# Moving the second half's layer-norm work behind the first index list

## The reference

```python
h = h + attn(_layernorm(h), ...)
x = _layernorm(h).reshape(-1, D)                 # second layer norm
gate_logits = x @ gate_weight.T                  # 16 experts
top_vals, top_idx = jax.lax.top_k(gate_logits, 2)
routing_w = jax.nn.softmax(top_vals, axis=-1)
mask = any(top_idx == arange(E))
hid = jax.nn.silu(einsum('td,efd->tef', x, w1))  # per chosen expert
h_mean = sum over the tokens of an expert / counts
y_mean = einsum('ef,edf->ed', h_mean, w2)
out = einsum('tk,tkd->td', routing_w, y_mean[top_idx])
```

## Time and profile before

| | us |
|---|---|
| median of 3 runs | 421.34 |
| lowest, highest | 420.61, 424.37 |
| profiled execution, its own span | 501.4 |
| first gather starts, in that span | 200.03 |
| first expert product starts | 252.03 |

### The profile page before, as it was taken

One profiled execution on the slowest core, in us unless ns is written; L12 is line 12 of the kernel. 1 busy time (PEld: TensorE's weight loads), 2 busy tenths in 40 slices (PEclk: granted clock), 3 DMA queues, 4 the chain that ended last, 5 costly groups with the idle time before them and its releaser, 6 DMA issues.

```text
span 501.4 us, 7310 instructions
## 1 busy us (share of the span) xinstructions
PE 397.6 (79%) x1929; PEld 269.9 (54%) x1930; DVE 311.4 (62%) x827; ACT 218.1 (43%) x423; POOL 205.3 (41%) x231
## 2 busy tenths in 40 slices
PE   8999999998898987554591404589987877899984
PEld 7888888886898974423440101244433433344552
DVE  3598888888788999543530101577744543577884
ACT  3334555445232666536350101456644443567320
POOL 2011111115400998757467775400066666610510
PEclk9999999998998996756587556799999788999998
DMA  6206533322209350647312111100291111100029
GB/s 182 66 1 164 139 86 109 102 80 82 81 1 262 98 140 2 193 140 212 106 57 52 54 52 43 31 0 2 54 331 47 37 47 42 47 16 1 1 73 251
DMA packets 53020, 43.68 MB, mean 87 GB/s; under 512 B 20686, under 2 KB 45980, under 8 KB 52732
## 3 DMA queue, kind: packets, MB, share of 16 engines
q1 hardware_dynamic: 44276, 32.09, 22.3%
q0 software_dynamic: 4416, 9.05, 6.5%
q10 hardware_dynamic: 4296, 2.15, 1.6%
HBM read 34.86 MB, written 8.42 MB: 86 GB/s over the span
## 4 chain that ended last, share of the span: by engine, by line
PE 47%; DVE 19%; issue 12%; another core or an unknown queue 10%; ACT 6%; POOL 3%; DVEq 2%; ACTq 0%; POOLq 0%
PE P L662 16%; PE P L935 14%; PE P L867 6%; ACT P L1265 4%; DVE BIG L1712 3%; DVE H L1828 2%; PE P L905 2%; PE P L1062 2%; PE P L697 2%; PE P L655 1%; POOL XN L597 1%; DVE arena L1504 1%; POOL arena L594 1%; PE P L688 1%
## 5 line engine op out<-in xcount | busy, mean ns | idle before, releaser
L1712 DVE TENSOR_TENSOR BIG<-BIG,P 128x512 f32 x138 | 95.0, 688 | 115.9 <-issue 75.1
L935 PE MATMUL P<-w1T,arena 128*128 x276 | 142.4, 652 | 12.0 <-DVE BIG L1712 8.7
L935 PEld LDWEIGHTS P<-w1T,arena 128*128 128x128 f32 x276 | 52.6, 209 | 67.1 <-issue 66.4
L1254 ACT COPY arena<-P 128x384 f32<-128x384 f32 (+1 forms) x48 | 22.4, 467 | 119.6 <-remote 50.4
L1265 ACT ACTIVATE P<-P 128x512 f32<-128x512 f32 x138 | 72.8, 580 | 1.6 <-PE P L935 1.5
L614 POOL DMA_INDIRECT XN<-table,arena x60 | 58.1, 968 | 30.1 <-issue 18.1
L614 POOL DMA_INDIRECT arena<-table,arena x42 | 39.7, 946 | 57.9 <-PE P L935 40.8
L557 POOL TENSOR_TENSOR rs<-ve,mhalf 123x4 f32<-123x4 f32 x16 | 17.6, 1098 | 101.9 <-DVE ve L1356 101.9
L1103 ACT ACTIVATE arena<-P 128x492 f32<-128x492 f32 x48 | 27.9, 583 | 50.6 <-PE P L662 50.5
L614 POOL DMA_INDIRECT BIG<-table,arena x36 | 34.6, 960 | 24.7 <-remote 12.4
L905 PE MATMUL P<-ident,XN 128*128 128x128 f32 x60 | 11.4, 304 | 41.6 <-issue 35.3
(11 more groups left out here) (242 smaller groups left out, 639.7 us busy)
## 6 DMA issues: line engine op xcount, KB each, us to landing
arena<-kpad SPq DMA_DIRECT2D x16, 492.0 KB, 4.0
XN<-in_L_ffn_w SPq DMA_DIRECT2D x1, 4096.0 KB
arena<-in_x SPq DMA_DIRECT2D x16, 224.0 KB
table<-XN SPq DMA_DIRECT2D x4, 896.0 KB
BIG<-table SPq DMA_DIRECT2D x1, 2048.0 KB
out<-H SPq DMA_DIRECT2D x8, 224.0 KB
out<-H ACTq DMA_DIRECT2D x8, 224.0 KB
BIG<-table SPq DMA_DIRECT2D x1, 1024.0 KB
```

Of the source, the lines that this page charges most:

```text
L935: mm = nc.tensor.matmul(bank[:, :], stat, w1T[:, bass.ds(e * FF, FF)], start=True, stop=True)
L1254: nc.scalar.copy(GTs[:, bank, 0:count * SLOT], PT[:, 0:count * SLOT]).then_inc(GT_ready, 1)
L1712: v.tensor_tensor(at, at, bank[:, :], ALU.add).then_inc(esum_step, 1)
```

## The change

Statistics, moments and bias of quarters 2 and 3 leave the first list's part of DVE's program and stand in and behind the searches of quarters 2 and 3. The bias of quarter 0 (`shift(0)`) moves from ahead of the first search to behind it. POOL computes the factors of quarters 2 and 3 between gathers, ahead of gathers 8 and 18, and the eight rows of quarter 2 that it normalised go to ACT. ACT normalises all 32 rows of quarters 2 and 3 in the second list's part. PE's `ranks(0)` moves one n up, `ranks(1)` and `totals` two.

```diff
-NORM_POOL = (8, 8, 8, 0)
+NORM_POOL = (8, 8, 0, 0)
+        RSTD_AT = (8, 18)
@@ POOL
-            def norms(g):
+            def rstd_of(g):
                 pool.wait_ge(ve2_ready, g + 1)
                 qb = slice(g * QB, (g + 1) * QB)
                 nc.gpsimd.tensor_tensor(rs2[0:T, qb], ve2[0:T, qb], mhalf[0:T], ALU.pow).then_inc(rstd2, 1)
+
+            def norms(g):
                 pool.wait_ge(rstd2, g + 1)
...
-            norms(0)
+            rstd_of(0)
...
+            rstd_of(1)
+            norms(0)
             norms(1)
-            norms(2)
-            norms(3)
...
+                    if n in RSTD_AT:
+                        rstd_of(QA + RSTD_AT.index(n))
                     if n in paces:
@@ PE
                 x2_transposes(n)
-                if n == 11:
+                if n == 10:
                     ranks(0)
-                if n == 15:
+                if n == 13:
                     counts_behind(1, 0, 2)
+                if n == 14:
+                    ranks(1)
+                    totals(1, 2 * QA)
                 if n >= 1:
                     logits(n - 1)
-            ranks(1)
-            totals(1, 2 * QA)
@@ ACT
             copy_V(1)
-            for b in NORM_ACT[2]:
-                norm2(b)
             for m in range(2, 8):
                 copy_w1T(m)
-            for b in NORM_ACT[3][:6]:
-                norm2(b)
             code_OH(2)
...
             for m in range(10, 12):
                 copy_w1T(m)
-            for b in NORM_ACT[3][6:]:
+            for b in NORM_ACT[2]:
                 norm2(b)
             code_OH(3)
             copy_bits(3)
             low_onehots(3)
+            for b in NORM_ACT[3][:6]:
+                norm2(b)
             copy_V(3)
+            for b in NORM_ACT[3][6:]:
+                norm2(b)
             for m in range(12, E):
                 copy_w1T(m)
@@ DVE
             moments2(1)
-            shift(0)
-            top2(0, more_stats(2))
-            for b in range(2 * QB + (4 * 11 + 2) // 3, 3 * QB):
-                bn(b)
-            counts(0)
-            moments2(2)
+            top2(0, nothing)
+            shift(0)
             shift(1)
-            top2(1, more_stats(3))
-            for b in range(3 * QB + (4 * 11 + 2) // 3, 4 * QB):
-                bn(b)
+            def count_first(i):
+                if i == 2:
+                    counts(0)
+
+            top2(1, count_first)
             counts(1)
-            moments2(3)
...
-            shift(2)
...
-            shift(3)
             tile_ends(NA)
-            top2(2, nothing)
+            top2(2, more_stats(2))
+            for b in range(2 * QB + (4 * 11 + 2) // 3, 3 * QB):
+                bn(b)
             counts(2)
+            moments2(2)
...
+                if i == 10:
+                    shift(2)
+                if i not in (5, 7, 9):
+                    for b in range(3 * QB + 2 * i, min(3 * QB + 2 * i + 2, 4 * QB)):
+                        bn(b)
             top2(3, between)
             counts(3)
+            for b in [58, 59, 62, 63]:
+                bn(b)
+            moments2(3)
...
             low_onehots(3, 1)
+            shift(3)
             second_list()
```

## The result

The changed kernel takes 433.26 us (median of 4 runs, 433.02 to 433.37); the kernel before, in runs on the same chip, 421.68 (420.61 to 424.37). The ratio is 1.0276 [1.0251, 1.03]. The prediction of 430.8 had the sign, and the time lies in its range. The 11.6 us lost match the upper of the two sums in the prediction (+11.6), not the middle of 9.5 that it took.

What follows compares the result with a forecast made beforehand. Gathers, started from the second list, were taken as the bound, 2 us ahead of PE's tiles. Between +7.4 with gaps staying and +11.6 in full it took 9.5: 421.34 + 9.5 = 430.8 us, range 423.5 to 435.5.

Steps and rivals of the forecast that it cites:

- the upper of the two sums: Delay of gather 32 with the whole sum of steps standing, no gaps hiding any: +11.6 us.
- the middle of 9.5: End delay taken between +11.6 us and +7.4 with gaps staying, since gaps are probably in the timed runs in part.
- The path of the second list: DVE, PE and ACT steps from first list to codes and tiles: delays sum to +11.7 us, or +7.5 with gaps.
- The first list: DVE, ACT and PE up to gather 0: the late bias delays PE, first list and gather 0 +2.5 us.
- the relief of DVE: Statistics and moments leaving DVE's first-list part: 5.7 us less work, 1.85 per search, lost to waits for PE.
- the slack: 12.2 us of waits between gathers hide POOL's powers; gaps on ACT and DVE hide up to 4.2 us.
- 1.9 more than `copy_V(3)`: Gather 32 waits for the table's last write, 11.1 us behind that copy where it stood 9.2 behind.
- A, the relief wins: Rival: DVE alone bounds the first list, up to 5.7 us earlier; 3 to 5.7 us faster, 416 to 418; chance 0.07.
- B, mostly hidden: Rival: the first list's 2.5 us stay, the rest falls into gaps and waits; 0 to 4.2 us, about 424; chance 0.16.
- C, heavier: Rival: gathers resume slowly behind each power, 1.3 us twice, and PE's clock falls; 434 to 437; chance 0.15.
- The port rule: Moved DVE moments could block GpSimd's DMA descriptors and lengthen gathers, at most 3.9 us; the sum took nothing.

Runs made afterwards that it cites:

- before_again: The kernel before, unchanged, profiled a second time: 421.97 us, span 420.2.
- a_shift0: The changed kernel with the bias of quarter 0 put back ahead of the first search: 429.08 us, ratio 1.0197 to the kernel before.
- a_early_pow: The changed kernel with both powers ahead of gather 0, raised from quarter 1's variance: 432.62 us, ratio 1.0278 to the kernel before.
- b_q3_late0: The kernel before with only quarter 3's statistics, moments, bias, power and six ACT rows moved later: 423.52 us, ratio 1.0039.
- a_few_rows: The changed kernel with 30 of ACT's 32 normalised rows left out: 433.85 us, ratio 1.0303 to the kernel before.
- b_two_pows: The kernel before with two idle powers added to POOL's stream ahead of gathers 8 and 18: 427.89 us, ratio 1.0148.

## Why the prediction came out as it did

Undisturbed stamps of both kernels, beside the prediction's terms (us):

| | before | changed | moved | predicted |
|---|---|---|---|---|
| ACT's copy for n = 7 | 168.84 | 172.88 | +4.0 | +3.55 |
| gather 0 | 200.80 | 203.58 | +2.8 | +2.5 |
| PE, `ranks(2)` | 205.94 | 209.97 | +4.0 | +3.1 |
| PE, bits of quarter 2 | 211.51 | 217.96 | +6.5 | +5.2 |
| ACT, `copy_bits(3)` | 226.05 | 234.82 | +8.8 | +7.6 |
| ACT, `copy_V(3)` | 232.23 | 242.97 | +10.7 | +9.7 |
| first expert product | 240.22 | 253.17 | +13.0 | +11.7 |
| gather 32 | 242.88 | 253.42 | +10.5 | +11.6 |
| last gather | 375.17 | 386.67 | +11.5 | |
| span | 420.2 | 431.6 | +11.4 | +9.5 |

**The path of the second list** was right step by step: every row down to the first expert product is late by what the prediction added, and by a further 0.3 to 1.3 us. Gather 32 is the exception, 1.1 less late than predicted.

**The first list** was right in its sum, +2.5 against +2.8, but from two terms that were both too small. The windows of PE in the changed kernel (us, busy, granted clock, DMA share, GB/s):

```profile
170.00:173.00 3.00, 0.77 (x8) 1.00 0.00 0
173.00:175.00 2.00, 1.52 (x10) 0.77 0.04 8
175.00:177.00 2.00, 2.00 (x12) 0.50 0.00 0
```

and PE's rows, the first logits behind the wait and the ranks of quarter 0:

```profile
173.48 1.48 PE L710 MATMUL P<-gateT,arena 128*123 128x112 f32 x8 [2.71 <-ACT arena L1201]
...
177.77 0.19 PE L743 MATMUL P<-oneb,BIG 123*128 123x1 bf16 x2
```

PE stood 2.71 us for the copy, and then the granted clock fell to 0.50, the 1.2 GHz level. `logits(7)` starts at 173.48, 3.7 later than in `before_again` (3.05 were predicted). From there to the ranks at 177.77 it took 4.29 us, where two groups at full clock take 2.54: 1.75 us that the sum didn't have. Wait and clock together are 4.46. In `a_shift0`, where the bias stands early, the ranks come at 173.17, 4.60 sooner, and gather 0 comes 4.63 sooner. Against that stands the relief of DVE, 1.85 us there, where the prediction gave nearly nothing back.

**The step that failed** is the slack. The prediction read 12.2 us of waits between gathers and 15.4 us of gaps in the one profile it had, and wrote that beside them the powers are hidden and "the second list decides"; for the same reason it took 9.5 and not the full sum, since "the gaps are probably in the timed runs in part". `before_again`, whose span fits the timed runs, has none of them. Before, the gathers alone bound gather 32, with no wait in 42.08 us. So gather 32 pays 2.8 us for gather 0, 2 x 2.85 = 5.7 for the powers, 1.7 for the table (2.01 less the usual 0.30) and 0.3 for longer gathers: the 10.5 measured.

Behind gather 32 another 0.9 come. The stretch to the last gather lasts 132.3 us before and 133.3 now, and the step between its gathers, the few long ones left out, is 1.250 us in `before_again` and 1.259 in the changed kernel: 0.009 over 105 gathers is 0.9. The step is 1.256 to 1.261 in every undisturbed profile with two powers in the stream, and 1.248 to 1.250 in every other, among them `a_early_pow` (none) and `b_q3_late0` (one). So these 0.9 us go with the two late powers too: in `a_early_pow` gather 32 stands where it stood and the last gather starts 1.25 us sooner. What lengthens the steps isn't known.

That the total still met the full sum of +11.6 was partly luck. The sum let gather 32 move by 1.9 more than `copy_V(3)`, from 9.2 us behind it to 11.1. The 9.2 were read from the disturbed profile: in `before_again` gather 32 stands 10.65 behind `copy_V(3)`, held by the stream and not by this path, and now 10.45, so it moved by 0.2 less. What this term had too much, the steps behind gather 32 and the larger delays of the list made up.

There are two ways to gather 32, the stream with its powers and the list with ACT's rows and the table's write. They come out 1.7 us apart in the changed kernel, though only the second was summed as binding. `a_early_pow` and `a_few_rows` show both: each holds gather 32 at 253.2 without the other, in `a_few_rows` with the later gather 0 named there.

**Rivals.** A, the relief wins: half its mechanism is there (1.7 to 1.85 us earlier list once the bias is back), but not its price of 3 to 5.7, since PE and not DVE then limits the first list, as `a_shift0` shows ahead of `counts(1)`; and in the changed kernel the bias turns it around.

```profile
180.32 0.16 DVE L1574 CAST arena<-P 128x2 bf16<-128x2 f32 x1 [2.90 <-PE P L743]
```

B, mostly hidden, needed the gaps and falls with them. C, heavier: the lower clock is real, the slow start of gathers behind a power is not (1.02 and 1.05 long, 0.19 idle), and 433.26 stays just below its bounds. The port rule that the prediction weighed shows no difference between the kernels: what gathers 0 to 32 last beyond 0.95 us each sums to 2.1 us before and 2.3 after. The moved moments lengthened nothing (the gathers beside them, at 210.27 and 228.23, last 0.94 and 0.95); it is other rows that do, below.

## What to carry to other kernels

Before taking slack out of a profile, see that its span fits the timed runs. The one that was 80 us too long agrees with the second to 0.8 us at gather 0, and from there holds waits also where nothing looks odd, and these seemed to hide exactly what a moved instruction costs. Moving work "into gaps" of another engine needs the chain of in-order neighbours: a bias of 0.17 us went behind a search, two rows and a copy stood behind it, and PE lost 2.7 us and then 1.75 more by its clock. When two paths reach the same point within a microsecond or two, undoing one cause alone shows nothing; undo them together and one by one before calling either harmless.

## What the runs showed of the hardware

**The time around the span.** The changed kernel's profiled execution has 433.37 us against a span of 431.6, `before_again` 421.97 against 420.2: the span is 1.8 us shorter than the device time. The first profile of before was 80.1 longer than the median of its runs, with 0.70-us steps for register records.

**Gathers beside a two-input instruction of DVE.** In every undisturbed profile a few gathers behind the first last 1.2 to 2.0 us and not 0.95. In the profiles looked at they lie beside the long `TENSOR_TENSOR` rows of DVE (123x1024). POOL and DVE of the changed kernel, and of `b_two_pows`:

```profile
219.44 1.67 POOL L617 DMA_INDIRECT XN<-table,arena  x1 [0.30 <-issue]
221.41 1.48 POOL L617 DMA_INDIRECT XN<-table,arena  x1 [0.30 <-issue]
```

```profile
219.07 1.22 DVE L1605 TENSOR_TENSOR arena<-iotb,arena 123x1024 bf16<-123x1024 bf16 x1
...
220.86 1.22 DVE L1605 TENSOR_TENSOR arena<-iotb,arena 123x1024 bf16<-123x1024 bf16 x1
```

```profile
226.64 1.73 POOL L614 DMA_INDIRECT XN<-table,arena  x1 [0.30 <-issue]
...
231.52 1.87 POOL L614 DMA_INDIRECT XN<-table,arena  x1 [0.18 <-issue]
```

```profile
226.34 1.22 DVE L1602 TENSOR_TENSOR BIG<-iotb,arena 123x1024 bf16<-123x1024 bf16 x1
...
231.28 1.22 DVE L1602 TENSOR_TENSOR BIG<-iotb,arena 123x1024 bf16<-123x1024 bf16 x1
```

The first gather starts 0.37 us into a row of 1.22, so 0.85 is left of it, and it is 0.72 longer than usual; the next has 0.67 left and is 0.53 longer; the two of `b_two_pows` have 0.92 and 0.98 left and are 0.78 and 0.92 longer. Each time the gather grows by what is left of the row less some 0.1 us. The Trainium skill ("SBUF — State Buffer", on who takes the shared port pair, section "Who interferes with whom" and the summary) says that a DVE instruction with two SBUF inputs contends with a GpSimd instruction that reads SBUF, and that the one that issues second is blocked until the first ends. The four gathers agree with it, if a gather counts as such an instruction. The other order doesn't. Where the DVE row starts inside a gather, as here in `before_again`, it isn't blocked and lasts its 1.22:

```profile
212.34 1.06 POOL L614 DMA_INDIRECT XN<-table,arena  x1 [0.31 <-issue]
```

```profile
212.50 1.22 DVE L1599 TENSOR_TENSOR arena<-iotb,arena 123x1024 bf16<-123x1024 bf16 x1
```

No run moved a DVE row alone, so all this is seen, not tested.

**A power between gathers.** The step from the gather ahead of a power to the one behind it is 4.10 us in the changed kernel, at both places, where a step is 1.25: 2.85 us for an instruction of 2.94 or 2.95, hidden by nothing.
